# Sharing out 128 column copies anew between ScalarE and VectorE, and moving the second list load of each

## What is computed

```python
h_nodes = mlp2(x, node_W1, node_b1, node_W2, node_b2)      # mlp2: silu(h @ W1 + b1) @ W2 + b2
h_edges = mlp2(edge_attr, edge_W1, edge_b1, edge_W2, edge_b2)
msg_in = concatenate([h_nodes[dst], h_nodes[src], h_edges], axis=-1)
msgs = mlp2(msg_in, msg_W1, msg_b1, msg_W2, msg_b2)
agg = segment_sum(msgs, dst) / maximum(counts, 1.0)[:, None]
upd = mlp2(concatenate([x, agg], axis=-1), upd_W1, upd_b1, upd_W2, upd_b2)
out = layernorm(x + upd) * ln_g + ln_b
return layernorm(x + out)
```

## Time and profile before

| what | value |
|---|---|
| median of 3 runs | 4653.34 us (4652.77 to 4659.53) |
| the profiled execution | 4644.01 us, span 4642.2 us |
| busy: PE, PEld | 3236.5 us (70%), 2501.8 us (54%) |
| busy: ACT | 3221.5 us (69%) |
| busy: DVE | 2714.1 us (58%) |
| busy: POOL | 2695.8 us (58%) |
| DMA | 350.27 MB, mean 75 GB/s |
| mean granted TensorE clock | 0.688 of full speed |

### The profile page before, as it was taken

How to read it: one execution, slowest core, us unless ns; L and a number is a source line. 1 busy time by engine, 2 the same in 40 slices (tenths; PEclk the granted TensorE clock), 3 DMA queues, 4 the chain that set the end, 5 groups by cost and what they waited for, 6 DMA issues and landing times.

```text
span 4642.2 us, 96208 instructions
## 1 busy us (share of the span) xinstructions
PE 3236.5 (70%) x16224; PEld 2501.8 (54%) x16224; DVE 2714.1 (58%) x19337; ACT 3221.5 (69%) x24583; POOL 2695.8 (58%) x2848
## 2 busy tenths in 40 slices
PE   3576676777677777676777677677766777777765
PEld 2455555555555555555555555555555555555554
DVE  3556556556566565565565665664665655655656
ACT  2767777677777677777677777777676676776775
POOL 4555655555555556555555656555565555555562
PEclk7667767667767666667666767776677676666766
DMA  6233333333333333333333333333333333333331
GB/s 181 55 77 74 71 70 72 77 79 71 76 77 67 72 75 74 79 75 73 68 71 78 79 72 77 79 72 71 75 68 79 74 74 79 75 69 73 72 77 43
DMA packets 257342, 350.27 MB, mean 75 GB/s; under 512 B 105688, under 2 KB 193069, under 8 KB 246862
## 3 DMA queue, kind: packets, MB, share of 16 engines
q1 hardware_dynamic: 163340, 245.92, 24.5%
q0 software_dynamic: 91424, 95.97, 11.5%
q10 hardware_dynamic: 1954, 2.14, 0.1%
HBM read 330.76 MB, written 13.01 MB: 74 GB/s over the span
## 4 chain that ended last, share of the span: by engine, by line
ACT 59%; issue 30%; ACTq 4%; PE 4%; another core or an unknown queue 1%; DVE 1%; DMA 1%; SPq 0%; DVEq 0%
ACT colbuf L632 46%; ACT comb L717 12%; ACTq L617 3%; ACT msg L711 2%; PE p_pre L686 1%; PE p_pre L692 1%; ACTq L629 1%; PE p_hid L815 1%; PE p_sum L706 1%; DMA work<-in_xT 0%; PE p_hid L378 0%; ACT work L971 0%; ACTq L367 0%; PE p_pre L390 0%
## 5 line engine op out<-in xcount | busy, mean ns | idle before, releaser
L800 POOL DMA_INDIRECT b_ring<-b_table,src x2825 | 2673.4, 946 | 1837.5 <-issue 742.2
L632 ACT COPY colbuf<-shared 64x4 uint8 x22644 | 2380.8, 190 | 683.4 <-issue 662.3
L686 PE MATMUL p_pre<-wa_ring,comb 128*128 128x64 f32 x6250 | 1212.3, 365 | 1295.2 <-ACT msg L711 1054.5
L686 PEld LDWEIGHTS p_pre<-wa_ring,comb 128*128 128x128 f32 x6250 | 1127.1, 274 | 1558.1 <-issue 1556.8
L632 DVE COPY colbuf<-shared 64x4 uint8 x16001 | 1355.0, 183 | 525.7 <-issue 513.6
L902 DVE SCALAR_TENSOR_TENSOR comb<-shared,p_const 64x640 f32<-64x640 int32 x625 | 554.2, 887 | 1074.2 <-issue 562.5
L706 PEld LDWEIGHTS p_sum<-hot_ring,msg 128*65 128x65 f32 x6250 | 731.2, 205 | 253.6 <-issue 214.0
L815 PE MATMUL p_hid<-e_ring,w_e 128*128 128x320 f32 x1250 | 741.4, 690 | 54.9 <-ACT comb L717 39.0
L711 ACT ACTIVATE msg<-p_pre 128x320 f32<-128x320 f32 x625 | 273.5, 438 | 641.1 <-issue 606.9
L706 PE MATMUL p_sum<-hot_ring,msg 128*65 128x64 f32 x6250 | 711.5, 288 | 0.0
L717 ACT ACTIVATE comb<-p_hid,b_e 64x320 f32<-64x320 f32 x1250 | 652.5, 522 | 32.6 <-issue 20.3
(11 more groups left out here) (106 smaller groups left out, 574.1 us busy)
## 6 DMA issues: line engine op xcount, KB each, us to landing
e_ring<-in_edgeT SPq DMA_DIRECT2D x250, 320.0 KB
shared<-in_dst_row SPq DMA_DIRECT2D x125, 640.0 KB
b_ring<-b_table,src POOLq DMA_INDIRECT x2825
e_ring<-in_edgeT SPq DMA_DIRECT2D x50, 400.0 KB
shared<-in_dst_row SPq DMA_DIRECT2D x25, 800.0 KB
wa_ring<-a_table SPq DMA_DIRECT2D x625, 16.0 KB
work<-in_xT SPq DMA_DIRECT2D x25, 250.0 KB
work<-in_x SPq DMA_DIRECT2D x25, 250.0 KB
```

What stands on the lines that cost most here:

```text
L632: end = copy(colbuf[:, special % COLBUF, at:at + 1].bitcast(U8), of[j])
L686: return eng.matmul(p_pre[:, i % 2, k * H:(k + 1) * H], comb[:, i % COMBS, k * P:(k + 1) * P], wa_ring[:, i % RING, :], start=k == 0, stop ...
L800: eng.indirect_dma_start(b_ring[:, b_slot(i), k, :], None, b_table, bass.IndirectOffsetOnAxis(ap=src[:, u * TILES + k:u * TILES + k + 1], ...
```

## The change

The second register load of the list moves on both engines. On ScalarE it goes from ahead of the message to behind it. On VectorE the first part's load and copies go ahead of the one-hot, then come one-hot and addition, and behind them the second part's load and copies. The columns are shared 65 to 63 in place of 53 to 75, and a chunk has room for 32 words in either list.

```diff
-COLS = dict(vector=53, scalar=75)
+COLS = dict(vector=65, scalar=63)
...
-LOAD = dict(vector=32, scalar=40)
+LOAD = dict(vector=32, scalar=32)
...
             starts_a = loaded_columns(eng, "scalar", j + LEADIN, 0, 2)
             copied_columns(eng, "scalar", eng.copy, j + LEADIN, starts_a, 0, 2)
-            starts_a = loaded_columns(eng, "scalar", j + LEADIN, 1, 2)
             if i >= 1:
                 message(i - 1)
+            starts_a = loaded_columns(eng, "scalar", j + LEADIN, 1, 2)
             copied_columns(eng, "scalar", eng.copy, j + LEADIN, starts_a, 1, 2).then_inc(col_ok["scalar"], 1)
             step(i)
...
             if i + AHEAD < n:
                 comb_of(i + AHEAD)
-            hot_of(i)
             if j in (0, HALF_AT):
                 wait_alone(eng, list_in[j // HALF_AT], 32 * rr + 32)
             starts_v = loaded_columns(eng, "vector", j + LEADIN, 0, 2)
             copied_columns(eng, "vector", eng.tensor_copy, j + LEADIN, starts_v, 0, 2)
+            hot_of(i)
+            if i >= ADD_LAG:
+                add_sums(i - ADD_LAG)
             starts_v = loaded_columns(eng, "vector", j + LEADIN, 1, 2)
             copied_columns(eng, "vector", eng.tensor_copy, j + LEADIN, starts_v, 1, 2).then_inc(col_ok["vector"], 1)
-            if i >= ADD_LAG:
-                add_sums(i - ADD_LAG)
             step(i)
```

## The result

The changed kernel is slower: 4839.7 us (median of 4 runs, 4827.0 to 4841.9) against 4653.1 us (4 runs of the kernel before), a ratio of 1.039 with an interval of 1.037 to 1.041. The forecast was 4075 us, so the sign was wrong, not only the size. The profiled execution took 4827.0 us with a span of 4825.1.

A forecast was written before the change was run, and what follows sets the result against it. ScalarE's instruction stream was taken as the bound: 4.45 us clean plus 1.66 of stalls, 6.1, plus 0.15 for close engines; 6.25 x 625 + 160 = 4066 us, with 0.2% to the median 4075; range 3840 to 4500 us.

The forecast's parts named there:

- the sum of VectorE: VectorE's need a unit: 5.20 us now, plus 0.36 net, 0.2 for the addition, 0.1 for stalls, making 5.86.
- VectorE's clean parts: VectorE's undisturbed iteration from the comb's start: 3.96 us before, 4.32 after, net + 0.36 us.
- The wait of the addition: VectorE's addition, ahead of the second load, waits for TensorE's sums: 0.4 us at lower clock, 0.2 in the mean.
- ScalarE's part: ScalarE's clean iteration falls from 5.18 to 4.45 us, 0.73 less; fewer copies give 0.55 of it.
- The move of the load: ScalarE's second list load goes behind the message, which then directly follows the sixteenth copy, at 2.61 us.
- Stalls in proportion to instructions: ScalarE's stalls shrink with its instructions, 33.24 of 39: from 1.95 to 1.66 us a unit, ends 1.0 and 2.4.
- a supply that all engines share: Rival: a shared supply stalls the sequencers, so moving copies leaves 7.17 us a unit, 4653 us; chance 4%.
- The rival that came true: VectorE becomes the bound, its second load behind the addition's wait: 7.7 us a unit, 4980 us; chance 8%.
- the 1.97 us of slack: VectorE's waits a unit, 1.72 us ahead of the comb and 0.25 ahead of the addition, held against VectorE becoming the bound.
- POOL slowed by VectorE's copies: Rival: VectorE's added copies hold up POOL's gathers by 0.92 us a unit, 6.57 us, 4275 us; chance 3%.
- the indicators: Signs of a right forecast: copy counts, message behind copies, TensorE's second-layer idle some 700 us, comb's at most 250, VectorE's moved gap.
- those named for a wrong prediction: Signs: TensorE waits for the comb or addition; gathers over 1 us; ScalarE's idle time still above 1200 us.

## Why the prediction was wrong

**The step that failed** is the sum of VectorE: "Its need is 7.17 less what it waits ... so 5.20 ... Some 0.1 for more stalls. Need: 5.86", set against a ScalarE that was charged 1.66 us of stalls. Measured, VectorE needs 5.31 us a unit without stalls and its unit takes 7.46 with them: the 5.86 had room for some 0.55 us of stalls where about 2.1 came. Whoever subtracts an engine's waits from the period also subtracts the stalls that ran out while it waited. VectorE's wait ahead of the comb was real. Of its 1074 us, 562 are put down to "issue", but 478 of these end within 0.2 us, mostly 0.04 us, of the end of the second layer that the comb waits for, as nearly all of the 414 do that are put down to TensorE. From TensorE's and VectorE's timelines of the kernel before:

```profile
1718.55 1.30 PE L686 MATMUL p_pre<-wa_ring,comb 128*128 128x64 f32 x10 [1.93 <-issue]
1719.89 0.89 DVE L902 SCALAR_TENSOR_TENSOR comb<-shared,p_const 64x640 f32<-64x640 int32 x1 [1.66 <-issue]
...
1732.46 2.37 PE L686 MATMUL p_pre<-wa_ring,comb 128*128 128x64 f32 x10 [3.39 <-ACT msg L711]
1734.86 0.89 DVE L902 SCALAR_TENSOR_TENSOR comb<-shared,p_const 64x640 f32<-64x640 int32 x1 [2.80 <-PE p_pre L686]
```

So some 870 us were waits for TensorE, and TensorE waited for a ScalarE that stalled: the time was slack only as long as the stalls fell on somebody else's path. The two engines should have been compared on the same footing, clean to clean or stalled to stalled:

| us a unit | before: ScalarE | after: VectorE |
|---|---|---|
| no gathers, no stalls, whole kernel | 5.11 | 5.31 |
| stalls, (4653 less 3351)/625, two sessions | 2.08 | 2.08 |
| sum | 7.19 | 7.39 |
| measured, (time less 160)/625 | 7.19 | 7.49 |

The left column adds up by construction; the right one is the test, and it gives 0.2 of the 0.3 us a unit that were lost: the stalls are about as long whichever engine is the bound. The remaining 0.1 us of the right-hand column is not explained; the changed kernel's TensorE also runs at a lower granted clock (0.61, 0.69), but it has 1% of the chain.

**VectorE's clean parts** sum up right, 4.32 forecast and 4.23 to 4.53 measured, in part by luck. The first load was to hold the copies back until 1.30 us after the comb's start; they begin 0.91 behind it. The second load was to leave 0.1 us behind the addition and leaves 0.27 to 0.39. The wait of the addition, 0.2 us, was wrong: it idles for 2.4 us in all. What was left out is the node updates' place in a clean sum; they are up to 0.6 us a unit by busy time (3161.7 less VectorE's four groups above, over 625), and the mean unit without gathers lies 1.1 us above the clean 4.23.

**ScalarE's part** was half right. The 5.76 copies fewer are worth 0.57 us (4.94 to 4.37, the shortest common iteration of the kernel with the shares alone), forecast 0.55. The move of the load was worth 0.18 in my sum and is worth nothing. The "clean" iteration of the earlier trace rows wasn't: its 0.25 us ahead of the message, and a load that I took for the cause, don't come back in any undisturbed iteration. One iteration that looks clean, in a trace full of stalls, was too little to rest a term on.

**Stalls in proportion to instructions.** Taken from 1.95 to 1.66. They are some 2.1 us a unit in both kernels and go with the 4.5 indirect gathers of a unit, not with ScalarE's instructions. The rival that named "a supply that all engines share" fits what was seen (both engines often go on within 60 ns of each other) better than any other, and had 4%; that there is such a supply was not shown.

**The rival that came true** is the second: VectorE becomes the bound, which "decides above 7.17". Its price, 7.7 us, was close to the measured 7.46 for the wrong reasons (it charged the addition's wait and a bare first load); its chance of 8% followed from "the 1.97 us of slack", which was stalls for the most part. Free of stalls the two engines were, by an estimate, some 0.26 us apart before the change (4.94 and 4.68, as worked out ahead of the repeat of the shares; with more than 0.72 us for the updates it would be less): moving 4 columns gains 0.5%, where 1 to 2 were expected of it, and moving 12 loses 4%.

**POOL slowed by VectorE's copies** did not happen: the gathers' mean is 946 ns in both kernels, with 3623 copies more on VectorE. The reverse shows faintly: a VectorE copy's mean is 183 ns in the kernel before and 158 without gathers, ScalarE's 190 in both. The Trainium skill's page "SBUF — State Buffer" (section "SBUF: two separate sides") gives VectorE and GpSimd a shared port pair and says that ScalarE never waits for anyone; these rows agree with that. But ScalarE stalls as VectorE does, so by that section the shared ports aren't what stalls it. No run here tests the ports alone.

**Of the indicators**, the copy counts (19,020 and 19,624), ScalarE's message straight behind its copies in undisturbed iterations, and the comb's idle time (218 us, forecast at most 250) came as forecast; the last says little, for VectorE no longer waits once it is the bound. VectorE's gap was to lie ahead of its copies; it lies only ahead of the second part. TensorE's idle time ahead of the second layer is 200 us, not 700, with 871 us of another wait. Two of those named for a wrong prediction came: the addition is what TensorE waits for, and ScalarE idles for 1296 us ahead of copies and message.

## What to carry to other kernels

Compare the engines' needs on one footing: either take every engine's clean iteration and add the common stalls to the largest, or leave stalls out of all of them. Period less waits isn't a need when the engine waited for one that stalled. Before an idle time that is put down to "issue" is called a stall, look whether it ends at a fixed short distance behind the instruction that it should wait for; then it is a wait whose record is missing. Before moving work between two engines, work out how far apart they are, and move half of that; and when stalls end on two independent engines at once, look for what a third one does (here, remove its work and see) before sizing anything on them.

## What the runs showed of the hardware that was not expected

- In three of five sessions indirect gathers by GpSimd cost the whole core some 0.46 us each in the mean (1255 us over 2712 of them; the first 600 left out gave 1.06 each), though POOL wasn't on the chain; half the rows per gather changed it by 0.7%, and plain transfers of as many bytes on the same queue cost nothing (3357 us, 3351 without any). In the other two sessions the same kernel was 21% faster, and the kernels profiled there have at most 6 gaps among ScalarE's copies.
- While it stalls, the trace's records of semaphore updates come late as well: in the kernel before TensorE's for the source terms with a median of 1.0 us behind the end of its matmul, against 0.01 us where nothing stalls. Many are missing, too: the trace of the kernel before holds 24,939 of them, that with half the rows 22,283, those of the kernels without stalls and with as many transfers some 70,000, the one with plain transfers (70,746) among them. The kernel without gathers has 27,344, which is all, as 2712 gathers have 16 landings each (43,392). So stalls and lost records come together in every trace; which of them causes the other, or what causes both, is open. The Trainium skill's page "NOTIFIC — the notification-queue block" (section "Overflow: three behaviours, one of which stalls the engine") says that in one mode a full queue of trace records stalls whoever writes them, and that in others records are dropped or overwritten. The traces fit either in part; no run here shows or excludes that records are the cause.
- With stalls gone, 2825 gathers at 1.25 us are the next bound: 5.65 us a unit, and no edit to ScalarE or VectorE changed the time there by more than 0.15%.
